# Who scales the rows in the layer norms that end a stage: VectorE or GpSimd

## What is computed

```python
def _layernorm(x, axis=-1, eps=1e-05):
    m = jnp.mean(x, axis=axis, keepdims=True)
    v = jnp.var(x, axis=axis, keepdims=True)
    return (x - m) / jnp.sqrt(v + eps)

x = _layernorm(x + _L0_attn_ref(x, ...), axis=-1)
x = _layernorm(x + _L0_ffn_ref(x, ...), axis=-1)
...
x = _layernorm(x + _L3_ffn_ref(x, ...), axis=-1)
```

## Time and profile before

| | us |
|---|---|
| median of 3 runs | 2104.31 |
| lowest and highest | 2103.73, 2104.77 |
| the profiled execution | 2105.01 |
| its span, from its first instruction to its last | 2102.9 |

### The profile page before, as it was taken

The page is one execution under the profiler, slowest core; times in us unless marked ns, Lnnn a source line. Parts: engine busy times, 40 slices in busy tenths (PEclk is TensorE's granted clock), DMA queues, the critical chain, the costliest instruction groups (busy, mean ns, idle before and its releaser), DMA issues.

```text
span 2102.9 us, 28210 instructions
## 1 busy us (share of the span) xinstructions
PE 1962.9 (93%) x10552; PEld 1245.9 (59%) x10552; DVE 1089.8 (52%) x1971; ACT 775.4 (37%) x1647; POOL 747.5 (36%) x1203
## 2 busy tenths in 40 slices
PE   5899967999999999999999899979999997999897
PEld 3454435777777777777776687844444454544443
DVE  4666466555555555555555324135556354566345
ACT  1565523333333333333333233322455402565411
POOL 1455315434343434343432344322344312343300
PEclk9899979999999999999999899999999998999998
DMA  7223000101010101010100234115333006111101
GB/s 196 39 40 104 2 20 1 51 1 51 1 51 1 51 1 51 1 50 1 51 1 30 76 106 170 46 29 64 47 62 102 31 1 77 32 33 46 52 0 40
DMA packets 46200, 95.01 MB, mean 45 GB/s; under 512 B 7689, under 2 KB 35721, under 8 KB 43017
## 3 DMA queue, kind: packets, MB, share of 16 engines
q1 hardware_dynamic: 43474, 90.86, 16.9%
q10 hardware_dynamic: 2592, 2.36, 0.7%
HBM read 62.20 MB, written 2.10 MB: 31 GB/s over the span
## 4 chain that ended last, share of the span: by engine, by line
PE 83%; DVE 7%; ACT 2%; DMA 2%; issue 2%; POOL 1%; ACTq 1%; POOLq 0%; SPq 0%; DVEq 0%
PE PS L1365 11%; PE PS L1434 9%; PE PS L1417 7%; PE PS L1390 7%; PE PS L444 5%; PE PS L547 5%; PE PS L1776 5%; PE PS L525 5%; PE PS L491 5%; PE PS L572 3%; PE PS L1402 3%; PE PS L1376 3%; PE PS L1789 3%; PE PS L1747 2%; PE PS L459 2%
## 5 line engine op out<-in xcount | busy, mean ns | idle before, releaser
L965 ACT ACTIVATE PB<-PS 128x512 f32<-128x512 f32 x480 | 281.5, 600 | 240.6 <-PE PS L525 237.7
L741 DVE TENSOR_REDUCE NM<-PS 128x2 f32<-128x1024 f32 x192 | 209.2, 1091 | 185.7 <-PE PS L493 184.6
L870 POOL TENSOR_SCALAR_AFFINE_SELECT PB<-PB 128x256 f32<-128x256 f32 (+1 forms) x480 | 174.2, 367 | 322.9 <-ACT PB L965 316.9
L1564 ACT COPY PRT<-PS 128x512 f32<-128x512 f32 (+3 forms) x256 | 108.9, 426 | 415.6 <-PE PS L1402 409.8
L491 PE MATMUL PS<-KQ 96*128 96x512 bf16 (+3 forms) x768 | 189.1, 311 | 46.4 <-DMA KQ<-LOW 31.6
L1524 DVE TENSOR_REDUCE NX<-PS 128x1 f32<-128x512 f32 (+3 forms) x256 | 124.3, 490 | 171.2 <-PE PS L1391 169.2
L1677 POOL TENSOR_SCALAR PR<-PR,RCP 128x512 f32<-128x512 f32 (+3 forms) x256 | 135.7, 535 | 201.4 <-DVE RCP L1512 194.8
L525 PE MATMUL PS<-KQ 99*128 99x512 bf16 (+3 forms) x768 | 183.8, 305 | 5.6 <-DMA KQ<-NMT 2.5
L1390 PE MATMUL PS<-kT,qT 128*128 128x512 f32 (+3 forms) x512 | 184.0, 441 | 4.3 <-ACT PR L1622 4.1
L444 PE MATMUL PS<-XTT,WA 128*128 128x512 f32 x288 | 146.8, 617 | 13.5 <-DVE ident_masks_b L2314 12.0
L1622 ACT ACTIVATE PR<-PS,NX 128x512 f32<-128x512 f32 (+3 forms) x256 | 136.5, 533 | 46.9 <-DVE NX L1524 45.7
(11 more groups left out here) (285 smaller groups left out, 3965.7 us busy)
## 6 DMA issues: line engine op xcount, KB each, us to landing
KQ<-HI SPq DMA_DIRECT2D x90, 128.0 KB, 4.0
KQ<-MID SPq DMA_DIRECT2D x72, 128.0 KB, 4.7
WB<-f_w SPq DMA_DIRECT2D x12, 768.0 KB, 4.4
WB<-w1o SPq DMA_DIRECT2D x8, 1024.0 KB, 7.9
WC<-f_w SPq DMA_DIRECT2D x10, 768.0 KB, 4.4
WB<-w1a SPq DMA_DIRECT2D x8, 768.0 KB, 4.4
WB<-w1b SPq DMA_DIRECT2D x8, 768.0 KB, 5.9
WA<-w SPq DMA_DIRECT2D x6, 1024.0 KB, 6.4
```

The source lines that it names most:

```text
L741: x = dve.tensor_reduce(nm[:, h:h + 2, i], PS[:, b:b + 2, 0:(i + 1) * P], AX.X, ALU.max, negate=True)
L870: pool.affine_select(blocks, blocks, [[0, count], [1, P]], ALU.is_ge, 0.0, base=0, channel_multiplier=-1).then_inc(s16["probs_ready"].sem, 1)
L965: act.activation(PB[:, n % PBS, :], PS[:, 4 + n % 2, :], ACT.Exp, scale=self.scale)\
```

## The change

`finish` takes the engine as an argument, and `Tail` has a flag `pooled`. In a pooled tail GpSimd does `root(t)` and then `finish(t)`, tile by tile, and VectorE does the four `mean` alone and then waits for the last `s_x`. Pooled are the tails of sequence 1 in `a0`, `a1`, `Ffn1`, `a2`, `a3` and `Ffn3`, and both tails of `Ffn0`: 32 of the 64 row tiles. Both tails of `Ffn2` and the tails of sequence 0 elsewhere stay as they are. No wait is dropped: `slot_free` is the same, only the engine that signals `s_x` is another.

```diff
-            def finish(self, dve, u):
-
-                dve.wait_ge(self.s_r.sem, self.s_r.at(u + 1))
+            def finish(self, eng, u):
+
+                eng.wait_ge(self.s_r.sem, self.s_r.at(u + 1))
                 src = S[:, u % 2, :] if self.y or self.y_done else self.XB[:, u, :]
-                dve.tensor_scalar(self.XB[:, u, :], src, mv[:, u % 2, 0:1], rstd[:, u % 2, :],
+                eng.tensor_scalar(self.XB[:, u, :], src, mv[:, u % 2, 0:1], rstd[:, u % 2, :],
                                   ALU.subtract, ALU.mult).then_inc(self.s_x.sem, 1)
...
-                    if t >= 1:
+                    if t >= 1 and not self.pooled:
                         self.finish(dve, t - 1)
...
             def gpsimd(self, pool):
                 for t in range(NT):
                     self.root(pool, t)
+                    if self.pooled:
+                        self.finish(pool, t)
...
                 for t in range(NT):
                     self.tails[1].root(pool, t)
+                    self.tails[1].finish(pool, t)
                     if t == 2:
                         a1.x_low(pool, 0, (0,))
                 a1.x_low(pool, 0, (1, 2, 3))
...
                         self.tails[b].mean(dve, st, t, self.y_bank(b, t))
-                    if n:
-                        self.tails[(n - 1) // NT].finish(dve, (n - 1) % NT)
```

More of the change, by code:

```diff
@@ L191, in __init__ @@
             def __init__(self, b, y_tile=None, y_done=None, mul=None, add=None, times=1.0,
-                         last=False, banks=False, biased=None, after=None):
-                self.times, self.banks, self.b, self.biased = times, banks, b, biased
+                         last=False, banks=False, biased=None, after=None, pooled=False):
+                self.times, self.banks, self.b, self.biased, self.pooled = times, banks, b, biased, pooled
                 self.before = after
@@ L395, in __init__ @@
                 self.on["taken"] = self.on["turned" if rope else "rest_ready"]
-                self.tails = [Tail(b, self.y_tile, banks=True, biased=self.on["biased"] if bo is not None else None)
-                              for b in range(NB)]
+                self.tails = [Tail(b, self.y_tile, banks=True, biased=self.on["biased"] if bo is not None else None,
+                                   pooled=b == 1) for b in range(NB)]
                 self.b = 0
@@ L1137, in __init__ @@
             def __init__(self):
-                one = Tail(0, self.y_tile, times=2.0)
-                self.tails = [one, Tail(1, self.y_tile, times=2.0, after=one)]
+                one = Tail(0, self.y_tile, times=2.0, pooled=True)
+                self.tails = [one, Tail(1, self.y_tile, times=2.0, after=one, pooled=True)]
             def y_tile(self, pe, b, t):
@@ L1344, in __init__ @@
             def __init__(self):
-                self.tails = [Tail(b, banks=True) for b in range(NB)]
+                self.tails = [Tail(b, banks=True, pooled=b == 1) for b in range(NB)]
             def project(self, pe, p):
@@ L1757, in __init__ @@
                 one = Tail(0, y_done=(f1["down"], M1), mul=AD)
-                self.tails = [one, Tail(1, y_done=(f1["down"], M), mul=AD, after=one)]
+                self.tails = [one, Tail(1, y_done=(f1["down"], M), mul=AD, after=one, pooled=True)]
             def gate_up(self, pe, m):
@@ L2085, in __init__ @@
                 one = Tail(0, self.y_tile, last=True)
-                self.tails = [one, Tail(1, self.y_tile, last=True, after=one)]
+                self.tails = [one, Tail(1, self.y_tile, last=True, after=one, pooled=True)]
             def y_tile(self, pe, b, t):
@@ L2206, in vector @@
                         self.tails[1].mean(dve, st, t, PS[:, 4 + t % 2, :])
-                    if t:
-                        self.tails[1].finish(dve, t - 1)
                 dve.wait_ge(self.tails[1].s_x.sem, self.tails[1].s_x.at(NT))
```

## The result

The change makes the kernel slower: **2129.7 us** (2125.7 to 2130.8 in 4 runs) against 2104.0 (2103.7 to 2104.8 in 4 runs) of the kernel before, measured together. The ratio is 1.0114, with a 95% interval of 1.0101 to 1.0127. The forecast was 2099.1 with a range that ended at 2101.4. The profiled execution took 2130.8 us.

A forecast was written before the change was run, and what follows sets the result against it. TensorE holds 83% of the chain and VectorE 7%; only that 7% and idle pieces could move. Gains of 0.8 + 1.9 + 1.2 + 1.1 + 0.2 = 5.2 us off 2104.31 gave 2099.1 us, range 2096.6 to 2101.4.

The forecast's parts named there:

- the price of one GpSimd scaling: In the pooled tails: 0.70 us, from GpSimd's other 128x512 `tensor_scalar`, which scales `a1`'s attention weights by one column.
- upper bound: Price ceiling for GpSimd's moved scaling: 1.28 us, GpSimd's difference of two 128x512 tiles.
- Rival 1: GpSimd's scaling in the pooled tails costs more than 0.70; at 1.28 the kernel takes 2107.3 us, slower; chance 0.10.
- the turn that it worked out: Scaling price 1.12, where GpSimd needs 1.75 us a tile; beyond it each tenth costs 2.5 us, counted 25 times.
- `a1`, `a3` and `Ffn3`: Tails of these stages: `a1` -0.2 us with GpSimd setting the pace, `a3` -1.1, `Ffn3` 0.
- a late `y`: In `a0`, the fourth `y` on TensorE runs slowly and loses 0.48 of 1.31 us, leaving -0.8.
- `a2`: Tail of `a2`: -1.2 us, its last two turns left as slow as they were at a low clock.
- `Ffn0`: Tail over eight tiles, ended by GpSimd's last three `XLa` (3.89 us): over at 331.85 instead of 333.78, -1.9 us.
- Ffn1: Tail of `Ffn1`: 0, as TensorE's matmuls for `a2` leave 1.78 us to spare.
- third rival: Low-clock TensorE turns in the tails and at stage starts give back 2.0 us: gain 3.2, 2101.1 us; chance 0.10.
- Rival 2: GpSimd's scaling holds VectorE's statistics at the port, a round of 2.51 instead of 1.75: about 2111 us; chance 0.02.
- The broad rule: GpSimd and VectorE share an SBUF read port, so moving work might not help; result would be the second rival's.

The follow-up runs named there:

- the one-column experiment: The change with GpSimd's scaling as source * rstd * 1.0, leaving out the mean's subtraction in pooled tails; 2098.2 us against 2105.0 of the kernel before, ratio 0.9965.

## Why the prediction was wrong, step by step

**The step that failed** is the price of one GpSimd scaling: "I take 0.70 ...; only a second column is new." It was **2.08**. The second column was not the only new thing, and it costs 0.07. New was the pair of operations, subtract-multiply in place of multiply-multiply, and that costs 1.3 us. All of GpSimd's `tensor_scalar` in the kernel before, 256 of them, are the one line `L1677` with one pair, so the trace of before couldn't tell. The **upper bound** failed as well: 1.28, the price of a difference of two tiles, was thought to be above anything that reads only one tile. On GpSimd reading less is no bound: a single operation with one tile takes 1.56.

The root at 0.55, its shortest in the trace of before, was taken without a reason (the median was 0.78), and it came out right. The 0.78 were roots beside a scaling of VectorE, as that at 264.86 in `a0` before, and in the pooled tails VectorE has no scalings left.

**Rival 1, "dearer scaling", is what happened.** It had the mechanism (GpSimd becomes the pace) and the right slope; the turn that it worked out, at 1.12 us, no run lies close enough to test. With 2.08 its formula gives 1.0 - 25 x 0.96 = -23.0, or 2127.3 us, and 2129.7 was measured. Only its end at 1.28 and its chance of 0.10 were wrong. Worked out with 2.08, its terms meet the trace: a tail of four tiles 0.15 + 0.08 + 4 x 2.71 = 11.07 us from the first `ve` to the last scaling, measured 11.10 (`a0`, `a2`, `a3`) and 11.09 (`a1`); `Ffn3` +1.38, measured +1.39.

**Terms of the sum**, at the price assumed (the one-column experiment): `a1`, `a3` and `Ffn3` are within 0.1 us, and so is `a0`, but by luck: 0.48 was taken off for a late `y` that did not come late, and 0.45 was lost in a slow last turn that the term did not have. `a2` won 1.6 and not 1.2, since its last turn took 0.63 for four pieces, not the 1.03 that I left it. `Ffn0` won 2.2 and not 1.9; its last three `XLa` took 3.70 and not 3.89, with no scaling of VectorE beside them. The gain of 5.2 lies in the measured interval (0.0023 to 0.0046 of 2105 is 4.8 to 9.7 us). **Ffn1** was put at 0 with 1.78 us of cover, and came out at +0.3 though its last scaling was over 12.64 us after the first `ve`, 2.47 later than before (10.17): the cover hid most of it.

**Slow turns.** In the change the last turn of `a0` takes 1.09 us for four pieces, behind an idle time of 2.08:

```profile
272.10 0.63 PE L215 MATMUL PS<-ident_masks,XBB 128*128 128x128 f32 x4 [1.79 <-POOL XBB L264]
274.81 1.09 PE L215 MATMUL PS<-ident_masks,XBB 128*128 128x128 f32 x4 [2.08 <-POOL XBB L264]
```

That is the 0.46 by which `a0` grew more (3.44) than its scalings (11.10 - 8.12 = 2.98), and `a1` shows the same (1.09 in place of 0.63). It isn't a matter of the dear scaling alone: at the quick price the last turn of `a0` takes 1.08 too, behind an idle time of 1.15. So the third rival's slow turns were there in `a0`, but the opposite came in `a2`, where the last turn went from 1.03 to 0.63 behind that same idle time of 1.15. Over all tails the sum of the forecast lost nothing by it. What decides between the two lengths, these runs don't show.

**Rival 2**, that GpSimd's scaling holds VectorE's statistics, is refuted: `L255` took 694 ns in median and 696 at most over its 56 executions in the change. What the Trainium skill says in "SBUF — State Buffer", section Who interferes with whom (VectorE shares GpSimd's port only with two SBUF inputs or in a two-port mode), the trace bears out. In `Ffn1`, where `L250` has two SBUF inputs, three GpSimd scalings take 2.56 to 2.61, and the fourth, with VectorE idle, 2.08. So the port exists as a cost, 0.5 for each of three tiles in one stage, and `Ffn1` as a whole grew by 0.3. The broad rule that moving work between the two might not help came true in its result but not by its reason.

**The price again.** The rows give 0.77 for the quick form with 512 elements and 2.08 for the slow. The Trainium skill, "GPSIMD Engine Reference", section 3.1 Elementwise, gives 769 ns as the best case for 512 elements. The quick form with two columns, 767 ns, agrees with it. The quick forms with one column (0.69) and none (0.62) are below it, so here it is not the best case, and the measurement decides. The slow form is 2.7 times that figure, and the section doesn't set prices apart by operation.

**What would have caught it.** The prediction weighed "both are columns, and only one was measured" and looked at the operands only. The rival should have asked for everything in which the known row differs from the new instruction, the operation codes too, and where GpSimd is the engine should not have let another engine's, or another instruction's, price close the range above.

## What to carry to other kernels

Before work is moved to GpSimd, measure the very form, with its pair of operations and its operands, at its size: here 0.77 and 2.08 us stood behind the same instruction name, and by the prediction's sum the turn from gain to loss lies between them, at 1.16. If the form is slow, look for an equal one in a quick pair: x - m is x + (-m), and a 128x1 negation on VectorE turned +25.7 us into -6.2. An experiment that gives a moved instruction the price one assumed, even at the cost of the result, tells at once whether the plan or the price was wrong.

## What the runs showed of the hardware

- GpSimd's `tensor_scalar` at 128x512, float32: multiply-multiply, multiply-add and add-multiply 0.62 to 0.77 us; subtract-multiply, multiply-subtract, add-add, subtract-subtract and multiply-max 1.93 to 2.10; one operation alone 1.56 to 1.57. At 128x128: 0.30 to 0.45, 0.65 to 0.81 and 0.60 to 0.61. VectorE does subtract-multiply in 0.54 at 128x512.
- So on GpSimd "multiply by a column" is quicker written as multiply by the column and by 1.0 (0.69) than as a single multiplication (1.56).
- A column in place of a constant costs some 0.07 us at either size (0.62, 0.69 and 0.76 for none, one and two columns).
- An Identity activation of ScalarE from SBUF to SBUF with column scale and bias took 0.81 us at 128x512, its copies from PSUM 0.56 to 0.59.
- GpSimd is held up when VectorE reads two tiles from SBUF: its scaling took 2.6 us in place of 2.08 (1.23 in place of 0.77 in the quick form), its root 1.00 in place of 0.55.
- VectorE's own scaling, which reads one tile from SBUF, and GpSimd hold each other up too: in the kernel before, GpSimd's root took 0.78 beside it in place of 0.55, and the scaling itself 1.48 in place of 0.54 beside `XLa`. VectorE's statistics (`L255`) took 0.70 at most over the whole of both kernels.
